# Transposing the layer-norm tiles through four float32 PSUM slots in place of two bfloat16 ones

## The reference, cut to what matters

```python
x = L0_attn_x                                  # (2, 4096, 2048) float32
xn = _layernorm(x, axis=-1)                    # (x - m) / sqrt(v + 1e-5)
x = x + _L0_attn_ref(xn, ...) + _L0_ffn_ref(xn, ...)

# attention, its first line
h = x * jax.lax.rsqrt(jnp.mean(x * x, axis=-1, keepdims=True) + EPS) * norm_w
Q = _lora_proj(h, wq, qA, qB, lora_scale)      # K and V alike
# feed-forward, its first lines
x = fwht(x * SU_ug) / SCALE
x_up = x @ W_up.T * (Wscale_ug[:INTER] * SCALE)
```

## Time and profile before

| | |
|---|---|
| time of the kernel before, median of 2 runs | 3236.36 us (3236.07 to 3236.64) |
| time of the profiled execution | 3236.52 us |
| its span on the slowest core (core 6), from which all rows come | 3234.9 us |
| spans of the eight cores | 3213.8 to 3234.9 us |
| median of die 0, of die 1 | 3225.2, 3226.2 us |
| PE, PE weight load, DVE, ACT, POOL busy | 2425.7, 1193.4, 1207.5, 639.2, 278.7 us |
| mean granted TensorE clock of the eight cores | 0.863 to 0.866 |

### The profile page before, as it was taken

The page is one execution under the profiler, slowest core; times in us unless marked ns, Lnnn a source line. Parts: engine busy times, 40 slices in busy tenths (PEclk is TensorE's granted clock), DMA queues, the critical chain, the costliest instruction groups (busy, mean ns, idle before and its releaser), DMA issues.

```text
span 3234.9 us, 39122 instructions; the slowest of 8 cores (3213.8 to 3234.9 us)
## 1 busy us (share of the span) xinstructions
PE 2425.7 (75%) x12160; PEld 1193.4 (37%) x12160; DVE 1207.5 (37%) x2521; ACT 639.2 (20%) x1302; POOL 278.7 (9%) x389
## 2 busy tenths in 40 slices
PE   0368898456889999819992389755779999954998
PEld 0123366333334444304441134533334444421443
DVE  4645510664113345470003544166312434455000
ACT  4212221443111111100003022244201111100000
POOL 0000000000000000170000000000000000045000
PEclk9999999555989999959995599855789999976998
DMA  2055233000577777607752256500168888843674
GB/s 87 24 101 96 54 66 59 18 1 9 106 147 146 146 152 147 127 13 132 129 105 104 61 104 119 101 1 1 32 125 149 146 149 150 146 82 61 119 134 117
DMA packets 42062, 304.58 MB, mean 94 GB/s; under 512 B 5008, under 2 KB 5264, under 8 KB 5904
## 3 DMA queue, kind: packets, MB, share of 16 engines
q0 software_dynamic: 37264, 269.24, 46.5%
q1 hardware_dynamic: 4608, 32.83, 2.8%
HBM read 558.69 MB, written 12.58 MB: 177 GB/s over the span
## 4 chain that ended last, share of the span: by engine, by line
PE 66%; DVE 9%; issue 7%; DMA 6%; ACT 6%; POOL 4%; DVEq 0%; ACTq 0%; SPq 0%; POOLq 0%
PE pAB L1223 7%; PE pCD L1223 7%; PE pAB L1109 7%; PE pCD L1131 7%; PE pCD L1109 7%; PE pAB L1131 7%; PE pAB L702 5%; PE pAB L1005 4%; PE pAB L754 2%; PE pCD L754 2%; POOL bigA L1088 2%; POOL bigA L1083 2%; DMA warena<-wqT 2%; ACT parena L892 2%; DVE bigA L520 1%
## 5 line engine op out<-in xcount | busy, mean ns | idle before, releaser
L702 PE MATMUL pAB<-bigA,warena 128*128 128x512 bf16 x1280 | 296.4, 385 | 38.2 <-DVE kfm L734 16.0
L1223 PE MATMUL pAB<-bigA,warena 128*128 128x512 bf16 x512 | 126.8, 413 | 161.7 <-DVE bigA L1088 84.4
L1150 DVE TENSOR_TENSOR bigA<-parena 128x512 bf16<-128x512 bf16 x128 | 54.5, 425 | 421.6 <-ACT parena L1143 406.9
L1260 DVE TENSOR_TENSOR acc<-acc,pE 128x128 f32<-128x128 f32 x64 | 18.4, 288 | 494.5 <-PE pE L1254 493.2
L702 PEld LDWEIGHTS pAB<-bigA,warena 128*128 128x128 bf16 x1280 | 120.6, 99 | 195.5 <-issue 67.3
L1088 DVE TENSOR_TENSOR bigA<-bigA 128x512 bf16<-128x512 bf16 x316 | 180.2, 570 | 33.2 <-DVE bigA L1083 0.5
L1083 DVE TENSOR_TENSOR bigA<-bigA 128x512 bf16<-128x512 bf16 x314 | 176.6, 562 | 25.5 <-ACT bigA L1050 2.7
L507 PE MATMUL pT<-identb_s,parena 128*128 128x128 bf16 x192 | 22.4, 309 | 183.9 <-ACT parena L494 183.9
L1109 PE MATMUL pAB<-parena,warena 128*128 128x512 bf16 x512 | 121.4, 392 | 35.8 <-DMA parena<-x1scr 35.8
L1223 PEld LDWEIGHTS pAB<-bigA,warena 128*128 128x128 bf16 x512 | 52.7, 104 | 233.7 <-issue 183.7
L883 PE MATMUL pE<-identb_s,parena 128*128 128x128 bf16 x256 | 37.4, 300 | 125.4 <-ACT bigA L923 101.4
(11 more groups left out here) (168 smaller groups left out, 3825.4 us busy)
## 6 DMA issues: line engine op xcount, KB each, us to landing
warena<-wupT POOLq DMA_DIRECT2D x32, 1024.0 KB, 8.4
warena<-wgT POOLq DMA_DIRECT2D x32, 1024.0 KB, 11.0
vtm<-wupT POOLq DMA_DIRECT2D x32, 1024.0 KB, 8.7
vtm<-wgT POOLq DMA_DIRECT2D x32, 1024.0 KB, 11.1
warena<-wdT POOLq DMA_DIRECT2D x32, 1024.0 KB, 9.7
vtm<-wdT POOLq DMA_DIRECT2D x32, 1024.0 KB, 9.5
warena<-wqT POOLq DMA_DIRECT2D x16, 1024.0 KB, 9.6
warena<-wkT POOLq DMA_DIRECT2D x16, 1024.0 KB, 8.3
```

The lines of the kernel that those rows point to most:

```text
L702: h0=hc0, w_=w, sub_=sub: t.matmul(q_.ap[:, 0:w_], wchunk(s_, d_, 256, sub_ * 128)[:, 0:128], h_tile(d_, h0, w_), start=(d_ == 0), stop=Fa ...
L1150: tz = S.emit("vector", lambda v, m_=mt, pp=mt % 2: v.tensor_mul(z_tile(m_), gbuf(pp), ubuf(pp)), waits=[tu, tg] + zgate, inc="dve", force ...
L1223: ct_=ct, k_=k, r_=rhs_ap: t.matmul(q_.ap, wslot_ap(s_, jj_ * 256 + ct_ * 128, jj_ * 256 + ct_ * 128 + 128), r_, start=(k_ == 0), stop=(k_ ...
```

## The change

The transposes go through four slots of two banks each, in float32, and so take all eight banks:

- slot 0 is `pAB`, slot 1 `pCD`, slot 2 the whole of `pT` read as float32, slot 3 `pE` (blocks 0 to 3) with `pF` (blocks 4 to 7);
- PE makes a block by `t.matmul(block, source, identity)` with a float32 result in place of `t.transpose`;
- DVE copies each block with the same `tensor_scalar`, same destination, same scalar, and a float32 source;
- the readers of the old buffers are handed to the slots ahead of the stage, and the slots' readers back to the old buffers behind it.

The number and order of the instructions stays. The diff, cut (the part for `xn_buf` and `x0_tile` is the same as that for `hst_buf` and `h_tile`, with `su_a` as scalar):

```diff
-            ptq_rot = [pT0, pT1]
+            lng = [PBuf(), PBuf(), PBuf(), PBuf()]
+            lng[0].ap = pAB_t[:]
+            lng[1].ap = pCD_t[:]
+            lng[2].ap = pT_t[:].bitcast(F32)
+            lng[3].ap = None
+            lng[0].r = pA.begin_write() + pB.begin_write()
+            lng[1].r = pC.begin_write() + pD.begin_write()
+            lng[2].r = pT0.begin_write() + pT1.begin_write()
+            lng[3].r = pE.begin_write() + pF.begin_write()
+            ln_epf = (pE_t[:], pF_t[:])
             ptq_i = [0]
+
+            def ln_transpose_group(src_fn, waits0, emit_evac):
+                g = lng[ptq_i[0] % 4]
+                gi_ = ptq_i[0] % 4
+                ptq_i[0] += 1
+                wq_ = g.begin_write()
+                tpe = None
+                for k in range(8):
+                    if gi_ == 3:
+                        dst = ln_epf[k // 4][:, (k % 4) * 128:(k % 4) * 128 + 128]
+                    else:
+                        dst = g.ap[:, k * 128:(k + 1) * 128]
+                    tpe = S.emit("tensor", lambda t, d_=dst, s_=src_fn(k): t.matmul(
+                        d_, s_, identb_s[:], start=True, stop=True),
+                        waits=(waits0 + wq_) if k == 0 else [],
+                        inc="pe" if k == 7 else None)
+                g.set_w(tpe)
+                tev = None
...
+                    tev = emit_evac(k, psrc, tpe if k == 0 else None,
+                                    k == 7)
+                g.add_r(tev)
+                return tpe, tev
...
-                    q = ptq_rot[ptq_i[0] % 2]
-                    ptq_i[0] += 1
-                    wq_ = q.begin_write()
...
-                                     t.transpose(
-                                         q_.ap[:, k_ * 128:(k_ + 1) * 128],
-                                         hst_buf(pp)[:, f_ * 128:(f_ + 1) * 128],
-                                         identb_s[:]),
...
+                    def srcfn(k, h_=half, pp=par2):
+                        f = h_ * 8 + k
+                        return hst_buf(pp)[:, f * 128:(f + 1) * 128]
+
+                    def evac(k, psrc, wtok, is_last, h_=half, c_=hc):
+                        f = h_ * 8 + k
+                        return S.emit("vector", lambda v, f_=f, p_=psrc, cc=c_:
+                                      v.tensor_scalar(
+                                          h_tile(f_, cc, 128), p_,
+                                          normw_v[:, f_:f_ + 1], None,
+                                          op0=ALU.mult),
+                                      waits=[wtok] if wtok else [],
+                                      inc="dve" if is_last else None)
+                    tpe, tev = ln_transpose_group(
+                        srcfn, [th, t_idb] + gate_bigA, evac)
...
+            for bb, g in ((pA, lng[0]), (pB, lng[0]), (pC, lng[1]), (pD, lng[1]),
+                          (pT0, lng[2]), (pT1, lng[2]), (pE, lng[3]), (pF, lng[3])):
+                bb.r = list(g.r) + ([g.w] if g.w else [])
```

More of the change, by code:

```diff
@@ L406, in build_nc @@
                 gate_par = gate_bigA
-            ptq_rot = [pT0, pT1]
-            ptq_i = [0]
+            lng = [PBuf(), PBuf(), PBuf(), PBuf()]
[8 more added lines that the diff above has]
+            ln_epf = (pE_t[:], pF_t[:])
+            ptq_i = [0]
+            def ln_transpose_group(src_fn, waits0, emit_evac):
[15 more added lines that the diff above has]
+                tev = None
+                for k in range(8):
+                    if gi_ == 3:
+                        psrc = ln_epf[k // 4][:, (k % 4) * 128:(k % 4) * 128 + 128]
+                    else:
+                        psrc = g.ap[:, k * 128:(k + 1) * 128]
+                    tev = emit_evac(k, psrc, tpe if k == 0 else None,
+                                    k == 7)
+                g.add_r(tev)
+                return tpe, tev
             for i in range(n_tiles):
@@ L499, in build_nc @@
                 for half in range(2):
-                    q = ptq_rot[ptq_i[0] % 2]
-                    ptq_i[0] += 1
-                    wq_ = q.begin_write()
[L503 to L506, removed]
-                                     t.transpose(
-                                         q_.ap[:, k_ * 128:(k_ + 1) * 128],
-                                         hst_buf(pp)[:, f_ * 128:(f_ + 1) * 128],
-                                         identb_s[:]),
-                                     waits=([th, t_idb] + wq_ + gate_bigA)
-                                     if k == 0 else [],
-                                     inc="pe" if k == 7 else None)
@@ L514, in build_nc @@
-                    q.set_w(tpe)
-                    hstb[par2].add_r(tpe)
[L516 to L525, removed]
@@ L526, in build_nc @@
-                    q.add_r(tev)
+                    def srcfn(k, h_=half, pp=par2):
[10 more added lines that the diff above has]
+                                      inc="dve" if is_last else None)
@@ L530, in build_nc @@
                     for half in range(2):
[L531 to L544, removed]
@@ L545, in build_nc @@
-                        q.set_w(tpe)
-                        xnb[par2].add_r(tpe)
[L547 to L556, removed]
@@ L557, in build_nc, with srcfn, evac @@
-                        q.add_r(tev)
+                        def srcfn(k, h_=half, pp=par2):
+                            f = h_ * 8 + k
+                            return xn_buf(pp)[:, f * 128:(f + 1) * 128]
+                        def evac(k, psrc, wtok, is_last, h_=half, o_=oc):
+                            f = h_ * 8 + k
+                            w = [wtok] if wtok else []
+                            if k == 0:
+                                w.append(t1)
+                            return S.emit("vector", lambda v, f_=f, p_=psrc, oo=o_:
+                                          v.tensor_scalar(
+                                              x0_tile(f_, oo, 128), p_,
+                                              su_a[:, f_:f_ + 1], None,
+                                              op0=ALU.mult),
+                                          waits=w, inc="dve" if is_last else None)
@@ L558, in build_nc @@
+                        tpe, tev = ln_transpose_group(
+                            srcfn, [txn, t_idb] + gate_bigA, evac)
+                        xnb[par2].add_r(tpe)
                         x0_ready.append(tev)
+            for bb, g in ((pA, lng[0]), (pB, lng[0]), (pC, lng[1]), (pD, lng[1]),
+                          (pT0, lng[2]), (pT1, lng[2]), (pE, lng[3]), (pF, lng[3])):
+                bb.r = list(g.r) + ([g.w] if g.w else [])
             x1_toks = []
```

## The result

The changed kernel takes 3263.93 us (median of 11 runs, 3254.66 to 3451.15), the kernel before, in the same sessions, 3243.17 us (median of 10, up to 3555.65). Some executions of any kernel show a lower granted clock on the cores of one die and take some per cent longer; without them the medians are 3263.15 us (10 runs, up to 3271.31) and 3240.10 us (8 runs, 3234.67 to 3247.36), and it is on such runs that the ratios rest. The ratio is 1.0068, with a 95% interval of 1.0051 to 1.0084: slower by 0.68%, an interval that leaves out no change and lies within the 2% band. In us that is 22, where 21.4 us was forecast.

A forecast was written before the change was run, and what follows sets the result against it. The layer-norm stages were taken as bound by a series ring, DVE and ACT in turn. 3236.5 us plus 21.4 for slower copies, all other terms 0, gave 3257.9 us, range 3250 to 3264.

The forecast's parts named there:

- a ring in series: Layer-norm stages: ACT, PE and DVE pieces follow one another, 14.09 us a tile, 19.21 us an own tile.
- Step 1: Four transpose slots in place of two remove PE's waits, at most 12.4 us, off the path; taken as 0.
- Step 2: Layer-norm transposes as matmuls with float32 result: gain or cost at most 0.9 us; taken as 0.
- Step 3: DVE's layer-norm copies from float32 cost 67 ns more each, 21.4 us over 320 copies (bounds 0 and 25.0).
- the upper bound of 78 ns: Highest extra price of one DVE copy, from pitches: 0.270 us, including 0.070 for the scalar, against 0.192.
- Step 4: Nothing hides the slower copies, on the path in all 12 tiles; the whole 21.4 us should reach the end.
- keep their lengths: Sign of being right: stages behind the first Hadamard matmul, itself 12.8 us later in the first pass, stay as long.
- A: Rival: DVE's copies already run at the slow rate, so no change, 3237 us; chance 0.08.
- B: Rival: PE's waits for layer-norm slots were on the path, so faster, 3224.1 us; chance 0.01.
- C: Rival: unbroken transposes raise PE's clock until the Hadamard matmuls, 5.1 us back, 3252.8 us; chance 0.04.
- D: Rival: copies' fixed part grows as PE writes other slots; 3261.5 us at 78 ns a copy; chance beyond that 0.04.
- the base of the sum: Whole kernel: profiled execution of 3236.5 us, 0.16 us above the median of runs shown, to which the cost was added.

The follow-up runs named there:

- e1: Four slots as in the changed kernel, but blocks stay bfloat16 by transpose; ratio to the kernel before 0.9988, stages 211.77 us.
- e2: Float32 blocks by matmul as in the changed kernel, but only two slots; ratio to the kernel before 1.0063, stages 233.20 us.
- e5: Kernel before with layer-norm tiles emitted in a new, overlapping order, two slots, bfloat16; ratio to the kernel before 0.9769, stages 140.90 us.
- e7: New overlapping order of layer-norm tiles with four slots and bfloat16 blocks; ratio to the kernel before 0.9751, stages 141.11 us.
- e3: Changed kernel with constants in place of the copies' two scalars read from memory; ratio to the kernel before 1.0003, stages 213.75 us.
- e4: Kernel before with constants in place of the copies' two scalars from memory; one comparable run, no ratio, stages 195.08 us.
- e6: Changed kernel (four slots, float32) with layer-norm tiles in the new overlapping order; ratio to the kernel before 0.9789, stages 155.04 us.

## Where the prediction was right, and the step that failed

- **What bounds the stage.** Right: a ring in series, with DVE's copies in it and PE's slots beside it. The timeline after, e1 and e2 show it from both sides, and e5 shows that the order of emission closed the ring.
- **Step 1, four slots worth 0.** Shown by e1 (0.09 us in the stage) and, for an open ring, by e7 (0.2 us).
- **Step 2, the matmul at no cost.** DVE starts its copies 1.12 us after PE's first transpose, as before, and the sum of the stages leaves no room: 21.20 us against 320 x 66 ns = 21.1. L431 takes 306 to 312 ns on `pAB`, `pCD` and `pT`, against 309. No run changed the matmul and kept the copies; the cost is bounded by these sums alone.
- **Step 3, 67 ns a copy.** Measured 66 to 67, in duration (343 against 276) and in pitch (0.258 against 0.192). The construction by two rates and a fixed part was right, and the upper bound of 78 ns was too high because the scalar was: 70 ns from a comparison of L1121 with L658, which writes 16 partitions and not 128, where e3 and e4 show some 60. The 128-partition copy of the earlier trace rows, 690 ns with no scalar, would have given 748 - 690 = 58. The term taken does not hold the scalar, so the sum was not touched. The rule of the Trainium skill ("VectorE: DVE Perf Modes", "Why PSUM operands drop a tier") is borne out by the trace: 0.131 and 0.199 us with constants differ by 68 ns, against 66.7 for 64 columns at 1.04 ns. Of the two estimates that the prediction made from the table of the same page, 192 and 258 ns, both are now measured as pitches, but only with the scalar from memory; with a constant the pitches are 131 and 199 ns.
- **Step 4, nothing hides it.** 21.2 of 21.4 us reach the Hadamard matmuls, and nothing behind gives time back. That the stages behind "keep their lengths" held between the two layer norms, within 1 us; behind the second the profiled execution is 4.2 us longer.
- **The rivals.** A is out by e4. B is out by e1. C asked that the clock rise and stay up until the Hadamard matmuls. It did rise, and closer to them than the argument against it would have it, but these are at 587 ns, as before (see below). D is out: the copies are at 341 to 343 ns in all eight groups, below the 347 computed, although PE now writes other banks without a break.
- **The absolute time: the step that failed.** It is the base of the sum, 3236.5 us, with the sentence "so the same sum holds for the median", and the "some 2 us" that the range allows for stages that shift. Both took the spread of the kernel's time as nearly nothing, from two runs 0.6 us apart. The comparable runs of the kernel before spread over 12.7 us, from 3234.67 to 3247.36, with a median of 3240.10: the base lies at their low end, 3.7 us under it. The time is that of the slowest of eight cores, and which core that is, and by how much, is settled in the stages that the change does not touch: in the profiled execution these brought 5.2 us in the mean core, and 3.2 us between the mean and the slowest. So 3257.9 us became 3263.93 in the median and 3265.95 in the profiled execution, with a term of the change that was right within 1 us. Rival D reserved 0.04 for a price of the copies beyond its bound, and nothing was reserved for a base that is off. That the median still lies at 3264.0 or under, by 0.07 us, is luck.

## What to carry to other kernels

A wait of an engine on a buffer is worth something only if another engine on the path is late because of it: look at the idle time of the reader (0.0 at L551) before adding buffers for the writer. A wider PSUM type is not free where the copies out are on the path; here it cost 66 ns for each 128-column block and bought nothing. Where a profile shows a ring in series over several engines, the order of emission is worth a trial before any of its pieces is made faster: here it gave 71 us of the 212 in the two stages, three times what the copies' type had cost. And a forecast of an absolute time needs the spread of its base: a difference can be right within 1 us where the time is off by 6.

## What the runs showed of the hardware that was not expected

**The clock and its record.** The mean granted clock fell from 0.863 to 0.866 before to 0.846 to 0.857 after, and yet nothing ran slower. The busy times by stretch, 80 to 100 us, kernel before and changed kernel (the granted clock is the third figure from the end):

```profile
80.00:100.00 20.00, 4.00 (x34) 3.31 (x35) 10.12 (x44) 9.21 (x9) 0.00 (x0) 1.00 0.17 63
```

```profile
80.00:100.00 20.00, 3.35 (x32) 3.21 (x32) 11.97 (x42) 7.41 (x7) 0.00 (x0) 0.80 0.14 53
```

Before, the whole first stage reads 1.00, though the 128x512 matmuls behind it (L564) take the same 583 ns as behind the second stage, which reads 0.50. The trace's first record of the clock is at 192.8 us there (core 6), at 88.6 us in the changed kernel (core 3); up to it the page shows full speed, and the durations say half. After, the last four of an unbroken piece of 32 transposes, at 88.56, take 0.41 us, where the same four of the next tile take 0.63:

```profile
109.63 0.63 PE L431 MATMUL pF<-identb_s,parena 128*128 128x128 bf16 x4
```

From 92 us on the record reads 0.50. So the clock went up at the end of that piece for a moment, as rival C had it. It did so once more behind the last own tile, whose transposes end at 152.7: the stretch from 154 to 156 us reads 1.00, that from 157 to 160 us 0.50. The first Hadamard matmul starts at 158.76, less than 2 us after the clock was down again, and they all go at the old duration:

```profile
L583 PE MATMUL pAB<-bigA,h_s 128*128 128x512 bf16 x32 | 18.4, 587 | 17.8 <-DVE bigA L566 12.1 <-DVE bigA L587 5.5
```

e1, with bfloat16 transposes in one piece, has the lower mean as well (0.848 to 0.857), and e2, with float32 matmuls in three pieces, has the old one (0.863 to 0.864). The kernels in the new order agree: 0.863 to 0.866 in e5, with its pieces broken, and 0.852 to 0.858 in e6 and e7. It is the unbroken piece that moves the record, not the float32 result.

**The scalar read from memory** costs 59 to 61 ns of each 128-column copy in pitch, nearly as much as the type; in duration it is 42 to 71 ns, by die and by tensor.
